# A convolution and expert layer: second products one step later, three inner buffers, two routing banks

## What is computed

```python
def metaformer(x):
    x = x + conv_branches(layernorm_over_channels(x))      # four dilated filters, projection, group norm, relu
    t = to_tokens(x)                                       # 2 x 9216 tokens of 256
    t = t + moe(layernorm(t))
    return from_tokens(t)

def moe(tokens):                                           # 8 experts, the top 2 for each token
    probs = softmax(tokens @ router_w.T)
    rw, re = top_k(probs, 2)
    rw = rw / rw.sum(-1)
    combine = zeros((N, E)).at[arange(N)[:, None], re].set(rw)
    out = tokens
    for e in range(E):
        h = gelu(tokens @ w1[e] + b1[e])
        out = out + combine[:, e:e + 1] * (h @ w2[e] + b2[e])
    return out
```

## Time and profile before

| | |
|---|---|
| Median of 3 runs | 2249.96 us (2245.78 to 2255.39) |
| The profiled execution | 2248.74 us |
| Its span, first to last instruction | 2246.9 us |
| Mean granted TensorE clock | 0.923 |
| Busy: PE, PEld | 1910.4 us (85%), 1832.1 us (82%) |
| Busy: DVE, ACT, POOL | 1560.9 us (69%), 1333.7 us (59%), 1083.1 us (48%) |
| The chain that ended last, by engine | PE 46%, ACT 14%, DVE 13%, POOL 9%, issue 7%, DMA 7% |

### The profile page before, as it was taken

How to read it: one execution, slowest core, us unless ns; L and a number is a source line. 1 busy time by engine, 2 the same in 40 slices (tenths; PEclk the granted TensorE clock), 3 DMA queues, 4 the chain that set the end, 5 groups by cost and what they waited for, 6 DMA issues and landing times.

```text
span 2246.9 us, 56560 instructions
## 1 busy us (share of the span) xinstructions
PE 1910.4 (85%) x20204; PEld 1832.1 (82%) x20204; DVE 1560.9 (69%) x4184; ACT 1333.7 (59%) x2877; POOL 1083.1 (48%) x1430
## 2 busy tenths in 40 slices
PE   5899799999969997999998895888888868999943
PEld 4899798999859997898888884888887768999932
DVE  4577675666556775777777774688887856777765
ACT  4677343333327774556556541887777758888822
POOL 3666212222215663145655562367777775555510
PEclk9999799999979998999999997898899989999965
DMA  4332597567554434677888879567667667888889
GB/s 143 105 106 78 145 294 189 141 173 174 153 142 133 132 102 111 190 228 216 227 232 245 237 209 322 171 219 227 224 218 225 202 192 274 284 282 283 280 310 368
DMA packets 341802, 459.87 MB, mean 205 GB/s; under 512 B 82677, under 2 KB 262709, under 8 KB 339173
## 3 DMA queue, kind: packets, MB, share of 16 engines
q1 hardware_dynamic: 231208, 246.52, 38.7%
q10 hardware_dynamic: 68433, 109.55, 14.9%
q0 software_dynamic: 41888, 100.18, 13.0%
HBM read 291.86 MB, written 174.69 MB: 208 GB/s over the span
## 4 chain that ended last, share of the span: by engine, by line
PE 46%; ACT 14%; DVE 13%; POOL 9%; issue 7%; DMA 7%; ACTq 3%; SPq 1%; POOLq 1%; DVEq 1%
PE ps_y L424 17%; PE ps_a L424 7%; PE ps_o L1050 6%; PE ps_b L987 4%; POOL expert_in L2148 4%; PE ps L424 3%; ACT w_now L1494 3%; POOL expert_out L2224 3%; ACT e_act L1483 3%; DMA o_acc<-res_scratch 3%; PE ps_tok L897 1%; DVE cat_lo L1938 1%; PE ps_o L1037 1%; ACT h_hi L1486 1%; DMA y_scratch<-y_acc 1%
## 5 line engine op out<-in xcount | busy, mean ns | idle before, releaser
L424 PE MATMUL ps_y<-cat_hi,wp 128*128 128x288 f32 x2048 | 483.5, 312 | 1.8 <-DVE cat_lo L1938 1.8
L2224 POOL DMA_INDIRECT expert_out<-e_out,e_dest x320 | 327.4, 1023 | 248.2 <-DVE e_out L2048 177.2
L2202 POOL DMA_DIRECT2D patches<-rows_scratch x340 | 190.4, 604 | 499.3 <-PE ps_o L1037 301.4
L424 PEld LDWEIGHTS ps_y<-cat_hi,wp 128*128 128x128 f32 x2048 | 354.4, 195 | 2.0 <-DVE cat_lo L1938 2.0
L2148 POOL DMA_INDIRECT expert_in<-r_ln,r_pos x288 | 290.0, 1007 | 106.3 <-issue 86.3
L2168 POOL TENSOR_TENSOR taps<-taps,g_rows 96x108 f32<-96x108 f32 (+2 forms) x416 | 243.8, 611 | 162.5 <-ACT g_rows L1310 158.6
L1379 ACT ACTIVATE bands<-ps_b 112x288 f16<-112x288 f32 (+4 forms) x256 | 105.1, 411 | 345.4 <-PE ps_b L987 331.9
L424 PE MATMUL ps_y<-cat_lo,wp 128*128 128x288 f32 x1024 | 308.1, 301 | 0.0
L424 PE MATMUL ps<-w,h_hi 128*128 x1280 | 258.5, 301 | 53.9 <-DVE h_lo L2037 51.1
L1938 DVE SCALAR_TENSOR_TENSOR cat_lo<-ps_o,cat_hi 128x288 fp32r<-128x288 f32 (+1 forms) x576 | 228.2, 419 | 92.9 <-ACT cat_hi L1385 89.4
L424 PE MATMUL ps<-e_hi,w_now 128*128 128x256 f32 x1280 | 266.1, 292 | 4.8 <-ACT w_now L1494 2.1
(11 more groups left out here) (201 smaller groups left out, 4488.3 us busy)
## 6 DMA issues: line engine op xcount, KB each, us to landing
e_x<-expert_in SPq DMA_DIRECT2D x160, 260.0 KB
patches<-rows_scratch SPq DMA_DIRECT2D x160, 192.0 KB
patches<-rows_scratch SPq DMA_DIRECT2D x256, 108.0 KB
patches<-rows_scratch SPq DMA_DIRECT2D x204, 112.0 KB
x_in<-in_x SPq DMA_DIRECT2D x48, 384.0 KB, 3.7
rows_scratch<-rows_st SPq DMA_DIRECT2D x48, 384.0 KB, 4.2
r_x<-in_x ACTq DMA_DIRECT2D x72, 256.0 KB
r_y<-y_scratch ACTq DMA_DIRECT2D x72, 256.0 KB
```

The lines of the kernel that those rows point to most:

```text
L424: mm = eng.matmul(out, lhs[p], rhs[q], start=start and n == 0, stop=stop and n == 2)
L2202: pool.dma_start(patch_target(s, n), patch_source(m, s, n)).then_inc(patch_pooled[s % RING], 16)
L2224: pool.indirect_dma_start(out=ys_dram, out_offset=bass.IndirectOffsetOnAxis(ap=e_dest[:, i, j:j + 1], axis=0), in_=e_out[:, u, j], in_offs ...
```

## The change

It does four things.

1. In step n TensorE does the second product of tile n - 2 (`BEHIND = 2`), VectorE's output follows suit, and GpSimd's scatters of the second image move up by one send (`- BEHIND`). After the last step two second products remain, not one.
2. `h_hi` and `h_lo` get three buffers (`HB = 3`). `e_act` keeps two; the gelu of tile n now waits until `h_lo` of tile n - 2 is made.
3. The second image's routing uses two PSUM banks, `ps_r[:, 0]` and `ps_r[:, 1]`, in turn. TensorE may turn a block when the copy before the last is made. The raw scores lie in two banks, so ScalarE copies them in two parts, 24 columns each.
4. One residual group less is loaded early (`EARLY = 4`), which frees the room for the third buffers.

```diff
-EARLY = 5
+EARLY = 4
+BEHIND = 2
+HB = 3
...
-        h_hi = sbuf(ctx, "h_hi", [128, 2, CC, S], F32R)
-        h_lo = sbuf(ctx, "h_lo", [128, 2, CC, S], F32R)
+        h_hi = sbuf(ctx, "h_hi", [128, HB, CC, S], F32R)
+        h_lo = sbuf(ctx, "h_lo", [128, HB, CC, S], F32R)
...
             def turn_tile(t):
 
                 j, k = divmod(t, BT)
+                bank, raw = (ps_k, t % TP) if t < ITILES else (ps_r[:, t % 2], t % TP // 2)
...
                 if k is not None:
-                    after(pe, r_kept, slots_before(r, k))
+                    after(pe, r_kept, slots_before(r, max(k - 1, 0) if r else k))
...
-                if n == 1:
+                if n == BEHIND:
                     pe.wait_ge(w_loaded_2, 16)
-                if n:
-                    second_product(n - 1)
+                if n >= BEHIND:
+                    second_product(n - BEHIND)
                 routing(1, 4 * n + 2)
                 routing(1, 4 * n + 3)
-            second_product(STREAM - 1)
+            for n in range(STREAM - BEHIND, STREAM):
+                second_product(n)
...
-                    last = act.activation(r_ln[:, p % HELD, k % TP, 0:C], ps_k[:, 0:C], ACT.Copy)
-                    if k % TP == TP - 1:
+                    bank = ps_r[:, k % 2] if r else ps_k
+                    last = act.activation(r_ln[:, p % HELD, k % TP, 0:C], bank[:, 0:C], ACT.Copy)
+                    if r and k % TP >= TP - 2:
+                        after(act, r_read, p - 1)
+                        odd = r_raw[:, p % 2].rearrange("p (k b e) -> p k b e", b=2, e=E)[:, :, k % 2]
+                        last = act.activation(odd, bank[:, 256:256 + TP // 2 * E].rearrange("p (k e) -> p k e", e=E), ACT.Copy)
...
                 act.wait_ge(e_first, n + 1)
+                after(act, h_lo_done, n - 1)
...
-                if n:
-                    output(n - 1)
+                if n >= BEHIND:
+                    output(n - BEHIND)
...
             def scatter_after(p, q):
 
-                return plans[1].placed(p) // 4 - 1 + q
+                return plans[1].placed(p) // 4 - BEHIND + q
```

More of the change, by code:

```diff
@@ L348, in build @@
             with ExitStack() as r2:
-                psum(r2, "routing", [128, 512])
+                ps_r = psum(r2, "ps_r", [128, 2, 512])
+            with ExitStack() as r2:
+                psum(r2, "first_routing", [128, 512])
                 ps_g = psum(r2, "ps_g", [128, 2, 256])
@@ L852, in rank_pair @@
             def rank_pair(p):
-                out = ps_k[:, 304:304 + (TP + 1) * E]
+                out = (ps_k if p < CPAIRS else ps_r[:, 0])[:, 304:304 + (TP + 1) * E]
                 pe.wait_ge(r_eith, p + 1)
@@ L1136, in second_product @@
                     for f in range(CC):
-                        mm = three_passes(pe, ps_2[:, u, j], [z[:, u, f, j * 128:(j + 1) * 128] for z in (h_hi, h_lo)],
+                        mm = three_passes(pe, ps_2[:, u, j], [z[:, n % HB, f, j * 128:(j + 1) * 128] for z in (h_hi, h_lo)],
                                           [w2[:, ds(e, 1), p, f * C:(f + 1) * C].rearrange("p o f -> p (o f)")
@@ L1230, in keep_slot @@
                         act.wait_ge(r_scattered[p % HELD], 16 * TP * TOP * (p // HELD))
[L1231 to L1232 removed]
+                    bank = ps_r[:, k % 2] if r else ps_k
[4 more added lines that the diff above has]
+                        last = act.activation(odd, bank[:, 256:256 + TP // 2 * E].rearrange("p (k e) -> p k e", e=E), ACT.Copy)
+                    elif not r and k % TP == TP - 1:
                         after(act, r_read, p - 1)
@@ L1239, in keep_slot @@
                     after(act, r_based, q)
-                    last = act.activation(r_count[:], ps_k[:, 304:304 + (TP + 1) * E], ACT.Copy)
+                    counted = ps_r[:, 0] if r else ps_k
+                    last = act.activation(r_count[:], counted[:, 304:304 + (TP + 1) * E], ACT.Copy)
                 if k < ITILES or ranked is not None:
@@ L1485, in hidden @@
                 act.wait_ge(e_act_done, n + 1)
-                act.activation(h_hi[:, u], e_act[:, u], ACT.Copy).then_inc(h_hi_done, 1)
+                act.activation(h_hi[:, n % HB], e_act[:, u], ACT.Copy).then_inc(h_hi_done, 1)
             def weights_hi(n):
@@ L2036, in hidden_lo @@
                 dve.wait_ge(h_hi_done, n + 1)
-                dve.tensor_tensor(h_lo[:, u], e_act[:, u], h_hi[:, u].bitcast(F32), ALU.subtract).then_inc(h_lo_done, 1)
+                dve.tensor_tensor(h_lo[:, n % HB], e_act[:, u], h_hi[:, n % HB].bitcast(F32), ALU.subtract).then_inc(h_lo_done, 1)
             def output(n):
@@ L2125, in _ @@
                     weigh_second(g)
-            output(STREAM - 1)
+            for n in range(STREAM - BEHIND, STREAM):
+                output(n)
             for g in range(GROUPS_OUT, 2 * GROUPS_OUT):
```

6 lines of the change are left out of this document (3 added, 3 removed).

## The result

The changed kernel takes 2254.85 us (median of 19 runs, 2244.98 to 2266.34) against 2247.9 us (19 runs, 2238.59 to 2256.88): ratio 1.0029, 95% interval 1.0016 to 1.0043. By that ratio it is 6.5 us slower, 3.6 to 9.7; the medians lie 6.95 apart. The profiled execution took 2255.11 us with a span of 2253.3, so its span is 6.4 us over the one of before.

What follows compares the result with a forecast made beforehand. It took GpSimd to bound the scattering, ScalarE's list with its issues the second image's stream, and transfers the tail. Terms -1.5 - 1.0 - 1.5 + 2.55 + 1.0 = -0.45 us gave a median of 2249.5 us, range 2238 to 2257.

Steps and rivals of the forecast that it cites:

- no change could be told: Whole kernel: changes within 0.5%, 11.2 us, cannot be told here; the outcome "same" had 81 in 100.
- the tail outweighs: Rival: last three sends and moved load cost 3.55 us, with no gains elsewhere 2253.5 us; 20 in 100.
- GpSimd bounds the scattering, so TensorE's waits are slack: Second image's scattering: GpSimd fills the stretch to 1.7 us, so TensorE's waits before the last scatter are slack.
- Head, -1.5: Steps 0 to 12, before the first scatter: a gain of 1.5 us, from nothing to 6.2.
- Scattering stretch, -1.0: While GpSimd scatters the second image: a gain of 1.0 us, from nothing to 1.7.
- Stream, -1.5: Changeover and second image's stream: a gain of 1.5 us of 0 to 6.05, bounded by ScalarE's waiting for TensorE.
- The end, +2.55: After the last first product: three sends queue on GpSimd, so tail loads begin 2.55 us later; bounds 1.4 and 2.6.
- The residual, +1.0: Tail: one 384 KB load moves there from the stream and costs 1.0 us; bounds nothing and 1.0.
- Second bank and copies, nothing beyond the head's term: Image 1's routing: removed bank waits worth nothing beyond the head's gain; 12 more ScalarE copies of about 0.2 us hidden.
- Half clock after the changeover: Rival: the 1.2 GHz stretch after TensorE's idleness grows by about three more tiles, giving 2261 us; 6 in 100.
- the other rivals: TensorE's waits on the path, 2176, 3 in 100; stream TensorE's, 2233, 5; small gains at bound, 2239.6, 12.

Runs made afterwards that it cites:

- pool_after: Changed kernel plus four small GpSimd writes after each portion of scatters; 2297.3 us, ratio 1.0222 to the kernel before.
- sp_after: Changed kernel with the first image's loads of outputs and residuals issued by SyncE instead of ScalarE; 2235.1 us, ratio 0.9940 to the kernel before.
- sp_pool: Kernel before with the first image's loads issued by SyncE and four small GpSimd writes per portion of scatters; 2275.4 us, ratio 1.0116.
- catchup152: Changed kernel with the second product one step behind again from step 152; ratio 0.9989 to the kernel before, on the slower kind of chip.
- catchup_2: Repeat of catchup152, the changed kernel with one step of distance again from step 152; ratio 0.9978 to the kernel before, slower kind of chip.
- sp_catchup: Changed kernel with the first image's loads issued by SyncE and one step of distance again from step 152; ratio 0.9913 to the kernel before, slower chips.
- early4: Kernel before with four early residuals in place of five, and padding so nothing else moves; ratio 1.0004, on the slower kind of chip.
- the two banks runs: Kernel before with only the two routing banks and the second raw-score copy, run twice on slower chips; ratios 0.9997 and 0.9989.

## Why the prediction was wrong

*Where it said no change could be told, there was one:* 0.29%, with an interval that leaves out zero. The time lies inside the range (2238 to 2257) and beside the rival "the tail outweighs" (2253.5), which had 20 in 100. Point by point:

- *GpSimd bounds the scattering, so TensorE's waits are slack:* right. 77.6 us of waits moved to other rows and the last scatter came 0.5 us earlier; pool_after adds 41.1 us for GpSimd's added work.
- *Head, -1.5:* 1.0 came, the same in all six traces of this kind of chip (63.0 against 64.0 us from the first `h_lo` to the first scatter). The first scatter stands at 1479.68 and 1479.69 all the same, because in this execution the convolution before it ended 1.0 us later; over the six traces the first `h_lo` lies between 1412.4 and 1417.3.
- *Scattering stretch, -1.0:* not seen. It is 0.5 shorter in this trace, but 354.6 in sp_after, and 1.2 longer in pool_after than in sp_pool.
- *Stream, -1.5:* this is the step that failed. "I take 1.5 of 0 to 6.05" looked only at how long ScalarE waited for TensorE and allowed no loss. The changeover did give something: the `h_lo` of tile 80 comes 0.3 to 0.8 us sooner after the last scatter. But from there to the `h_lo` of tile 159 every pair of traces is longer (+3.5, +0.9, and +3.1 with the loads off ScalarE), so that changeover and stream together were 2.8 us longer in this trace and 1.7 between the means of two traces of each order. The prediction had named ScalarE's list, issues included, as the bound of the stream, and then priced an issue at a constant 1.9 us a group. In this trace two issues of 2.5 and 2.7 us stand where the 1.6 and 2.1 us were lost. The issues of `o_y` are longer by 2 us a run with the new order on this chip and by 5 on average. Lengthened issues are not the whole cause, though: pool_after loses 0.9 us with issues as short as before's, and sp_after 3.1 with none of these loads on ScalarE. What else the order costs there is open. What would also have warned: a gain by removing a wait for `h_lo` is none on an engine that is not the bound.
- *The end, +2.55:* 3.0 in this trace, 2.75 between the means of three. Right in mechanism (five sends back to back, four before), and catchup152, catchup_2 and sp_catchup, with the old order from step 152, have the old distance of the second kind of chip.
- *The residual, +1.0:* 1.1 in this trace, 1.3 between the means of ten; early4 alone has 98.95 us. The two groups overlap (95.8 to 97.8 and 97.0 to 99.3). Right, somewhat too small.
- *Second bank and copies, nothing beyond the head's term:* the two banks runs agree (0.9997, 0.9989), and the head's 1.0 us is where the bank shows.
- *Half clock after the changeover:* the clock in the changeover is 0.89 (0.90 in the earlier trace rows), so the rival as it was priced is not seen. One piece at 1.2 GHz stands in the stream, the 3.4 us behind the long issue; it is inside the 1.6 us lost there. Of the other rivals none is seen.

For this trace the sum is -1.0 (head) - 0.5 (scattering) + 2.8 + 3.0 + 1.1 = 5.4 us, and the 1.0 of the convolution, which no code changed, makes the 6.4 of the span. The forecast had -0.45. Of the 5.85 between them 4.3 are the stream's term, which had the wrong sign, 1.0 the gains in head and scattering, and 0.55 the two costs, which were forecast well. That the time came out inside the range is the range's width and not the sum.

*Still open:* what holds an issue for 2.5 us. The Trainium skill's Perfetto Trace Analysis ("DMA Instruction — HWDGE (DVE, Sync)") says that the reported time of an issue includes waiting for exclusive use of the block that makes descriptors. The traces do not show it: none of the 37 issues of more than 1.1 us in the stream, in the 14 traces with these loads on ScalarE, overlaps an issue of SyncE. All 37 lie over one to three of GpSimd's sends, but so do 558 of the 635 shorter ones. On the second kind of chip the changed kernel may even be the faster (0.9975, up to 1.0002).

## What to carry to other kernels

Find the engine that bounds a stretch with its issues of transfers counted in, and then take no gain from a wait that another engine loses: of 77.6 us of waits 1.0 came back in the head and under 1 in the changeover. What such a change costs is at the ends, where a longer distance between stages leaves one more item in each queue behind it, and one constant (fewer early loads, for the memory) moves a transfer to where transfers bound. And a reordering can lengthen what it does not touch, here a few issues on another engine: leave a loss of a few us open in the range even where the sum shows only gains.

## What the hardware did that I had not expected

On four of the five chips the same program takes 2531 to 2546 us and not 2248. Some 127 to 146 us of the difference are there already at the first `h_lo`, so it is not of the expert stream alone. TensorE's granted clock is 0.76 in early4's stretch of scattering (0.91 in the earlier trace rows), and there are pieces in which TensorE starts a matmul only every 0.8 to 2.1 us while GpSimd issues indirect transfers back to back. 36 times four small writes on GpSimd, 31 us of added work, make the kernel before 46 us shorter there (0.9820), and the changed kernel 42 us longer on the first kind. A gain or loss measured on one chip need not hold on another: before trusting a ratio, compare the time of the kernel before.
